# The FFN stage of a BitNet-style transformer layer: the absolute maximum as a tree of max and min, and a subtraction moved from GpSimd to VectorE

## The reference, cut to what matters

```python
def act_quant(x):
    scale = 127.0 / jnp.clip(jnp.max(jnp.abs(x), axis=-1, keepdims=True), 1e-05)
    return jnp.clip(jnp.round(x * scale), -128, 127) / scale
...
h = bit_linear(x, w1)                                  # 1024 -> 4096
h = depthwise_conv1d(h.transpose(0, 2, 1), conv_w, conv_b)   # 3 taps over tokens
h = jax.nn.silu(h.transpose(0, 2, 1))
return bit_linear(h, w2)                               # 4096 -> 1024
...
x = x + _layernorm(_L0_attn_ref(_layernorm(x, axis=-1), ...), axis=-1)
x = x + _layernorm(_L0_ffn_ref(_layernorm(x, axis=-1), ...), axis=-1)
```

## Time and profile before

| | |
|---|---|
| median of 3 runs | 7791.81 us (7787.67 to 7802.6) |
| profiled execution | 7778.59 us, its span 7777.0 us |
| span of the cores | 7753.2 to 7777.0 us |
| mean granted TensorE clock of the cores | 0.695 to 0.699 of full speed |
| busy in the span | PE 48%, PEld 23%, DVE 56%, ACT 15%, POOL 9% |
| DMA, mean over the span | 32 GB/s |

### The profile page before, as it was taken

How to read it: one execution, slowest core, us unless ns; L and a number is a source line. 1 busy time by engine, 2 the same in 40 slices (tenths; PEclk the granted TensorE clock), 3 DMA queues, 4 the chain that set the end, 5 groups by cost and what they waited for, 6 DMA issues and landing times. The chain is left out here.

```text
span 7777.0 us, 57784 instructions; the slowest of 8 cores (7753.2 to 7777.0 us)
## 1 busy us (share of the span) xinstructions
PE 3694.5 (48%) x17510; PEld 1774.1 (23%) x17510; DVE 4360.3 (56%) x5860; ACT 1203.5 (15%) x1194; POOL 674.8 (9%) x630
## 2 busy tenths in 40 slices
PE   0688887221244344344416888872224444344341
PEld 0322222110132222222203222221112232232220
DVE  4344544557666666666653445445546666666665
ACT  0045655000000000000000455650000000000000
POOL 0000000000012112112110000000002112112111
PEclk9987877565566666666658887876656666676665
DMA  6200000113400000000042000001120000000004
GB/s 192 60 6 6 9 9 5 50 38 116 154 6 6 3 6 6 4 6 3 6 154 54 7 7 6 9 12 43 38 98 6 3 6 6 3 6 4 5 6 132
DMA packets 59119, 251.87 MB, mean 32 GB/s; under 512 B 6720, under 2 KB 6848, under 8 KB 55232
## 3 DMA queue, kind: packets, MB, share of 16 engines
q1 hardware_dynamic: 40992, 197.32, 8.1%
q0 software_dynamic: 17824, 50.86, 2.4%
HBM read 185.77 MB, written 67.11 MB: 33 GB/s over the span
## 5 line engine op out<-in xcount | busy, mean ns | idle before, releaser
L851 PE MATMUL s_hps<-s_xqfm,s_w1q 128*128 128x130 bf16 (+1 forms) x8192 | 865.1, 293 | 1143.7 <-DVE s_hgr L863 770.4
L534 ACT ACTIVATE s_pt<-s_sc 128x1024 bf16<-128x1024 f32 x1024 | 1048.9, 1024 | 697.1 <-PE s_sc L521 626.2
L851 PEld LDWEIGHTS s_hps<-s_xqfm,s_w1q 128*128 128x128 bf16 x8192 | 775.4, 134 | 1241.2 <-issue 1220.0
L969 PE MATMUL s_fp<-s_w2q,s_gq 128*128 128x512 bf16 x2048 | 716.7, 513 | 708.6 <-DVE s_gq L958 708.6
L521 PE MATMUL s_sc<-s_qa,s_ka 65*128 65x512 bf16 x2048 | 747.7, 456 | 144.4 <-ACT s_pt L534 25.4
L547 PE MATMUL s_atps<-s_pt,s_vsb 128*65 128x512 bf16 x2048 | 663.1, 420 | 0.0
L900 ACT ACTIVATE s_tcv<-s_tcv 128x4096 bf16<-128x4096 bf16 x32 | 115.7, 3617 | 3448.2 <-DVE s_tcv L898 3448.2
L952 DVE SCALAR_TENSOR_TENSOR s_f<-s_db,s_r 128x512 f32<-128x512 f32 x256 | 395.4, 1545 | 407.3 <-POOL s_db L949 407.3
L940 POOL TENSOR_TENSOR s_yb<-s_tcv,s_sgb 128x512 f32<-128x512 bf16 x256 | 295.9, 1156 | 3534.8 <-DVE s_sgb L926 3502.7
L863 DVE SCALAR_TENSOR_TENSOR s_hgr<-s_hps,iwcol,s_ivfm 128x130 bf16<-128x130 f32 (+1 forms) x1024 | 360.9, 352 | 430.2 <-PE s_hps L851 369.6
L969 PEld LDWEIGHTS s_fp<-s_w2q,s_gq 128*128 128x128 bf16 x2048 | 227.2, 119 | 1184.7 <-issue 1102.5
(11 more groups left out here) (121 smaller groups left out, 3766.9 us busy)
## 6 DMA issues: line engine op xcount, KB each, us to landing
s_xint<-x SPq DMA_DIRECT2D x64, 512.0 KB, 4.1
p0st<-w_t SPq DMA_DIRECT2D x8, 2048.0 KB, 9.0
p0st<-w_t SPq DMA_DIRECT2D x32, 512.0 KB, 3.8
x2scr<-s_x2t SPq DMA_DIRECT2D x32, 512.0 KB, 2.9
s_wst<-w_t SPq DMA_DIRECT2D x16, 1024.0 KB, 5.1
s_wst<-w_t SPq DMA_DIRECT2D x32, 512.0 KB, 3.8
fscr<-s_ft POOLq DMA_DIRECT2D x32, 512.0 KB, 3.0
s_frl<-fscr SPq DMA_DIRECT2D x32, 512.0 KB, 6.0
```

What stands on the lines that cost most here:

```text
L534: em.emit("scalar", lambda e, p=p, j=j: e.activation(pt[:, p * S + j * Q:p * S + (j + 1) * Q], scp[j][:], AF.Exp), waits=w)
L851: j0=j0, j1=j1, t0=t0: e.matmul(ps[:, j0:j1], w1q[:, dc * DH + cc * 128:dc * DH + cc * 128 + 128], xqfm[:, dc * S + t0 + j0:dc * S + t0 + j1],
L969: gq4=gq4, cc4=cc4: e.matmul(ps[:, nb * 512:(nb + 1) * 512], gq4[:, cc4 * 128:(cc4 + 1) * 128], w2q[:, cc * D + nb * 512:cc * D + (nb + 1) ...
```

## The change

Two edits within `_p5_ffn`. The single reduction L902 is replaced by a tree on DVE, once with max into `gmax` and once with min into `f12`, and one operation that joins the two as the larger of the maximum and the negated minimum. The tree works in a new bf16 tile `amx` of 1024 columns. In the quantise loop the difference `db2` is formed by DVE instead of POOL. `yb` gets two buffers, and POOL's multiply of group g waits for DVE's difference of group g - 2, the last reader of that buffer.

```diff
-        nc.sbuf_tensor(f"s{s}_yb", [128, 512], F32) as yb,
+        nc.sbuf_tensor(f"s{s}_yb", [128, 2 * 512], F32) as yb,
...
+        amx_cm = nc.sbuf_tensor(f"s{s}_amx", [128, 1024], BF16)
+        amx = amx_cm.__enter__()
...
-            em.emit("vector", lambda e: e.tensor_reduce(
-                gmax[:], rearr(tcv, "p (c t) -> p t c", c=HC), AX.X, ALU.max,
-                apply_absolute_value=True), waits=[(ac, None)])
+            for op, col in ((ALU.max, 0), (ALU.min, 1)):
+                em.emit("vector", lambda e, op=op: e.tensor_tensor(
+                    amx[:], tcv[:, 0:1024], tcv[:, 1024:2048], op),
+                    waits=[(ac, None)])
+                em.emit("vector", lambda e, op=op: e.scalar_tensor_tensor(
+                    amx[:], tcv[:, 2048:3072], 1.0, amx[:], ALU.mult, op))
+                em.emit("vector", lambda e, op=op: e.scalar_tensor_tensor(
+                    amx[:], tcv[:, 3072:4096], 1.0, amx[:], ALU.mult, op))
+                em.emit("vector", lambda e, op=op: e.tensor_tensor(
+                    amx[:, 0:512], amx[:, 0:512], amx[:, 512:1024], op))
+                em.emit("vector", lambda e, op=op: e.tensor_tensor(
+                    amx[:, 0:256], amx[:, 0:256], amx[:, 256:512], op))
+                em.emit("vector", lambda e, op=op, col=col: e.tensor_tensor(
+                    gmax[:, 0:128] if col == 0 else f12[:, 0:128],
+                    amx[:, 0:128], amx[:, 128:256], op))
+            em.emit("vector", lambda e: e.scalar_tensor_tensor(
+                gmax[:], f12[:, 0:128], -1.0, gmax[:], ALU.mult, ALU.max))
...
-            dg = 0
+            dve_rel = {}
             for g in range(8):
                 gq4 = gqb[:, (g % 2) * 512:(g % 2) * 512 + 512]
+                ybg = yb[:, (g % 2) * 512:(g % 2) * 512 + 512]
                 ts = tcv[:, g * 512:(g + 1) * 512]
-                yw = [(ac, silu_ac), (dv, sgb_dv), (ctx["gc"], dg)]
+                yw = [(ac, silu_ac), (dv, dve_rel.get(g - 2, sgb_dv))]
...
-                em.emit("gpsimd", lambda e: e.tensor_sub(db2[:], yb[:], r02[:]),
-                        inc=ctx["gc"], waits=[(dv, r0d)])
-                dg = ctx["gc"].n
+                em.emit("vector", lambda e, ybg=ybg: e.tensor_sub(
+                    db2[:], ybg, r02[:]))
+                dve_rel[g] = dv.n
                 em.emit("vector", lambda e: e.scalar_tensor_tensor(
-                    f12[:], db2[:], 1.5, r02[:], ALU.is_gt, ALU.add),
-                    waits=[(ctx["gc"], dg)])
+                    f12[:], db2[:], 1.5, r02[:], ALU.is_gt, ALU.add))
```

More of the change, by code:

```diff
@@ L932, in _p5_ffn @@
             silu_ac = ctx["ac"].n
-            dg = 0
+            dve_rel = {}
             for g in range(8):
                 gq4 = gqb[:, (g % 2) * 512:(g % 2) * 512 + 512]
+                ybg = yb[:, (g % 2) * 512:(g % 2) * 512 + 512]
                 ts = tcv[:, g * 512:(g + 1) * 512]
-                yw = [(ac, silu_ac), (dv, sgb_dv), (ctx["gc"], dg)]
+                yw = [(ac, silu_ac), (dv, dve_rel.get(g - 2, sgb_dv))]
                 if i >= 1 and g == 0:
                     yw.append((sf, fspill[i - 1]))
-                em.emit("gpsimd", lambda e, ts=ts: e.tensor_tensor(
-                    rearr_ap3(yb), rearr_ap3(ts), sgv, ALU.mult),
+                em.emit("gpsimd", lambda e, ts=ts, ybg=ybg: e.tensor_tensor(
+                    rearr_ap3(ybg), rearr_ap3(ts), sgv, ALU.mult),
                     inc=ctx["gc"], waits=yw)
                 yg = ctx["gc"].n
-                em.emit("vector", lambda e: e.tensor_copy(qi2[:], yb[:]),
+                em.emit("vector", lambda e, ybg=ybg: e.tensor_copy(qi2[:], ybg),
                         waits=[(ctx["gc"], yg)])
@@ L947, in _p5_ffn @@
                     r02[:], qi2[:], -1.0, None, ALU.add))
-                r0d = dv.n
-                em.emit("gpsimd", lambda e: e.tensor_sub(db2[:], yb[:], r02[:]),
-                        inc=ctx["gc"], waits=[(dv, r0d)])
-                dg = ctx["gc"].n
+                em.emit("vector", lambda e, ybg=ybg: e.tensor_sub(
+                    db2[:], ybg, r02[:]))
+                dve_rel[g] = dv.n
                 em.emit("vector", lambda e: e.scalar_tensor_tensor(
-                    f12[:], db2[:], 1.5, r02[:], ALU.is_gt, ALU.add),
-                    waits=[(ctx["gc"], dg)])
+                    f12[:], db2[:], 1.5, r02[:], ALU.is_gt, ALU.add))
                 ow = []
@@ L988, in _p5_ffn @@
         em.play()
+        amx_cm.__exit__(None, None, None)
     with (
```

## The result

The changed kernel takes 7627.22 us (median of 8 runs, 7624.24 to 7637.09); the kernel before took 7797.2 us in the runs beside it (7773.3 to 7830.93). The ratio is 0.9783, with a 95% interval from 0.9764 to 0.9802: 170 us faster, where 83 were forecast. The profiled executions differ by less, 7778.59 against 7624.8 us or 154 us, and their spans by 7777.0 - 7623.3 = 153.7.

A forecast was written before the change was run, and what follows sets the result against it. DVE's program order plus the POOL handoffs was taken to bound the quantise stretch. Subtraction -174.4, tree +91.5, meetings and clock 0 gave -83 us, so 7791.8 became 7709 us, with 8 in 10 for 7675 to 7770.

The forecast's parts named there:

- What bounds the kernel: FFN tiles: DVE's program order plus the POOL handoffs set the time; shortening that chain shortens the tile one for one.
- Part one: Quantise loop: moving the subtraction from POOL to DVE saves 0.68 us a group, -174 us in all.
- Part two: Quantise loop: two yb buffers change which DVE instruction POOL meets, seven meetings of 0.98 either way, 0 us; lower bound -220.
- rival 4: Quantise loop: meetings get cheaper with DVE ahead, half of the 220 us, giving 7599; chance 0.08.
- rivals in which POOL is shut out (1 and 2): Quantise loop: POOL loses the race now and then (7747, chance 0.15), or every multiply lies bare (7819, chance 0.12).
- rival 1: Quantise loop: POOL is kept out now and then, one of two multiplies lies bare, 38 us more, 7747; chance 0.15.
- Part three: Tile maximum: the tree takes 9.85 us where the reduction took 6.99, +2.86 us a tile, +92 us in all.
- Rival 3: Tile maximum: tree dearer, bf16 min steps at one column a cycle, 30 us more, 7739; both passes 7769; chance 0.05.
- Part four: DVE's wait for the last matmuls of a tile: TensorE's clock effect taken as 0, bounds -19 and +33 us.
- The sum: Whole kernel: -174.4 + 91.5 = -83 us from a median of 7791.8, giving 7709 us; chance 0.58.

The follow-up runs named there:

- three experiments: Old reduction restored in the changed kernel; two-input tree in the one-yb kernel; one-pass absolute-value tree in the changed kernel: 7541.35, 7560.36 and 7481.88 us.
- POOL first again: Changed kernel plus a one-column memset on VectorE between the subtraction and the first scalar-tensor-tensor: 7707.23 us, ratio 0.9893.
- half changes: Two runs: changed kernel with the old single reduction back, 7541.35 us; kernel before with only the tree added, 7880.64 us.
- the quantise loop alone: Changed kernel with the old single reduction back, keeping the subtraction on VectorE and two yb buffers: 7541.35 us, ratio 0.9676.
- the tree alone: Kernel before with the max and min tree in place of the reduction and nothing else: 7880.64 us, ratio 1.0123.
- one yb: Changed kernel with one yb buffer, POOL's multiply of group g waiting for VectorE's subtraction of group g-1: 7640.66 us, ratio 0.9811.
- the multiply on VectorE: Changed kernel with the multiply moved from POOL to VectorE too, POOL left out of the quantise loop: 7642.38 us, ratio 0.9793.

## Why the prediction was wrong

**What bounds the kernel.** Right. What was added to or taken from DVE's chain in the loop came out one for one in the loops' times (146 us for the change with its terms as measured, and 93, 88 and 151 us against 92, 86 and 149 expected for three experiments), but for the wait at the tile's end, which moved by itself.

**Part one, the subtraction.** Right. The last group, which meets nobody, shows it bare: from the cast's start to the end of the second scalar-tensor-tensor 4.02 us before (2746.76 to 2750.78), and 3.35 after (2827.42 to 2830.77). That is 0.67 us, where 0.68 were forecast.

```profile
core 7 of [0, 1, 2, 3, 4, 5, 6, 7], span 7777.0 us
start us, us, engine line op out<-in xcount [idle before <-releaser]
...
2746.76 0.43 DVE L944 CAST s_qi<-s_yb 128x512 int32<-128x512 f32 x1
...
2750.09 0.69 DVE L958 SCALAR_TENSOR_TENSOR s_gq<-s_db,s_f 128x512 bf16<-128x512 f32 x1
...
3430.68 1.16 POOL L940 TENSOR_TENSOR s_yb<-s_tcv,s_sgb 128x512 f32<-128x512 bf16 x1
3431.06 1.32 DVE L952 SCALAR_TENSOR_TENSOR s_f<-s_db,s_r 128x512 f32<-128x512 f32 x1 [1.93 <-POOL s_db L949]
```

(The last two rows are a meeting that part two comes to.)

Over the span it is the 407.3 us that L952 waited, less the 27.4 + 177.2 + 27.3 of the subtraction and the two gaps around it: 175 us.

**Part two, the meetings with POOL: the step that failed.** The prediction said: "If the two exclude each other, the order doesn't change the sum [...] Seven meetings of 0.98 before, seven after: **0 us**." They exclude each other, there are seven before and seven after, and the order does change the sum. Measured from POOL's start, the DVE instruction that it holds up effectively begins after a fixed time (its end less its own unhindered length):

| meeting | POOL's lead | effective start after POOL's start | cost to DVE |
|---|---|---|---|
| before, L952 | 0.03 us | 2719.94 - 0.69 - 2718.23 = 1.02 | 0.98 |
| POOL first again, L969 | 0.16 | 2835.66 - 0.69 - 2833.95 = 1.02 | 0.86 |
| changed kernel, the first cast | 0.20 | 2798.70 - 0.43 - 2797.26 = 1.01 | 0.81 |
| changed kernel, one L968 | 0.33 | 3839.22 - 0.69 - 3837.52 = 1.01 | 0.68 |
| before, one L952 | 0.38 | 3432.38 - 0.69 - 3430.68 = 1.01 | 0.63 |

The cast is met by the second multiply of the row marked x2, which starts 1.15 us before that row's end. The last two meetings are rare ones, in which DVE happened to start later than usual: 8 of the 1536 meetings of groups 2 to 7 on the eight cores of the changed kernel, and 40 of the 1792 meetings before. The one of the kernel before stands in the rows of part one, the one of the changed kernel is this:

```profile
core 5 of [0, 1, 2, 3, 4, 5, 6, 7], span 7623.3 us
start us, us, engine line op out<-in xcount [idle before <-releaser]
...
3837.52 1.16 POOL L957 TENSOR_TENSOR s_yb<-s_tcv,s_sgb 128x512 f32<-128x512 bf16 x1 [2.55 <-DVE s_db L965]
3837.85 1.37 DVE L968 SCALAR_TENSOR_TENSOR s_f<-s_db,s_r 128x512 f32<-128x512 f32 x1 [0.47 <-DVE s_db L965]
```

So POOL ahead costs some 1.01 us less its lead, be it the cast or the first scalar-tensor-tensor that it meets. With DVE ahead, L973's effective start lies 0.87 us behind the end of L968 (2806.60 - 0.69 - 2805.04), and DVE's own gap of 0.105 us is within those 0.87: 0.77. Against the 0.98 of before that is 0.21 us, of which 0.14 is that POOL is further on when it has been held up, and 0.07 is the gap that DVE would have had anyhow. By the rows' totals above that is 45 us in all. DVE first is not cheaper as such: from a lead of some 0.24 us (1.01 - 0.77) on, POOL first costs less, as the rare meeting at 0.33 shows within the changed kernel itself. In the kernel with POOL first again, 16 meetings on the eight cores still had DVE first, and they cost 0.77. With DVE first the instruction met was always the second scalar-tensor-tensor, so that another would lose the same 0.77 isn't shown. The prediction had the ends right (0 to -220) and rival 4 named the direction, at 110 us and 0.08. What it hadn't asked of a held instruction is whether it has already done part of its work when it is let in. That POOL does its first 0.14 us while it waits is an inference from these ends. POOL's own record bears it out: it ends at 2806.06, 1.02 us behind the end of L968, which is 0.14 less than its 1.16. But the profile doesn't show an instruction's inside.

The rivals in which POOL is shut out (1 and 2) fell: POOL got in at the first gap of DVE in every group in which it had work. (The handoff of 0.14 in rival 1 stands in rows 3, not in rows 6, which have 0.22 from L926 to L940.) The Trainium skill (SBUF — State Buffer, Who interferes with whom) says the blocked side waits for the whole instruction. In kind the trace agrees; but the cost here was 0.63 to 0.98 us for a POOL instruction of 1.16, and depended on who was first and by how much. The Trainium skill (SBUF — State Buffer, A bandwidth-pool intuition that's wrong) tells the 115 ns of a GpSimd transfer, not of an instruction like this one. Had they held here too, L973, ready 0.105 us behind L968, would have gone ahead of POOL. It didn't.

**Part three, the tree.** Right: 9.86 us a tile measured, 9.85 forecast, 92 us; 86 and 98 by the medians of the two half changes, 93 and 89 by their loops. Its dear part was named rightly too, the four scalar-tensor-tensor operations: without them 80 us less. Rival 3 fell.

**Part four, TensorE's clock.** Taken as 0 between bounds of -19 and +33, it came out at -18, at the favourable bound. Nothing in the prediction said which way it would go. The eviction's wait fell from 92.3 to 74.7 us in the profiles' slowest cores; over all eight cores it is 91 to 98 before and 75 to 77 after. The half changes say which edit did it: 74 to 75 us with the quantise loop alone, 88 to 96 with the tree alone. The last groups show what went with it. In the tile of the changed kernel shown above the last two follow each other unstretched, 3.45 us apart, and the eight matmuls of each take 1.89 us, the upper of TensorE's two levels. The tile shown of the kernel before ends with 1.89 too, so it is a matter of how often: of 256 evictions on the eight cores 97 waited less than 2.5 us before, and 212 in the changed kernel. In the four kernels with the last two groups unstretched the wait is 73 to 77 us on every core. Where only the last group is unstretched (before, the tree alone, one yb) or all groups are alike (the multiply on VectorE), it is 79 to 98, save two cores of one kernel at 76 and 78. That is a regularity over ten kernels, not a cause shown: no run spaced only the last groups.

**The sum.** 83 + 45 + 18 = 146 us, against 146 in the loops and 154 between the profiled executions. The medians differ by 170. The profiled execution of the kernel before (7778.6) lay near the low end of its runs, the changed kernel's (7624.8) amid its own, and those 16 us are scatter between executions that no run here explains. So of the 87 us between the forecast and the measured gain the meetings hold 45, the clock 18, the stages ahead of the first tile 8 and the scatter 16; the last two, and why the clock went that way, stay open. The range failed by this together: its low end took in the clock's bound but kept the meetings at 0. The meetings alone would have put the forecast at 7709 - 45 = 7664, and that too lies below the range of 7675 to 7770.

## What to carry to other kernels

Read off a meeting of two engines from both sides: what it costs each when it is second, since an instruction that is held can have part of its work behind it, and what counts is who starts first and by how much: here it was cheapest for VectorE to start first, unless GpSimd's lead was over some 0.24 us. Give work to a second engine only if the path's engine doesn't pay for it anyway: here a multiply of 0.80 us with its gap on VectorE was done by GpSimd at a price of 0.77 us to VectorE. And price a tree of operations by the form of each step: at 1024 bf16 columns a scalar-tensor-tensor took 1225 ns and a two-input step 692, and four of the former made the tree slower than the reduction it replaced, while one pass over values with the sign bit cleared made it faster.

## What the runs showed of the hardware that was not expected

- A POOL multiply of 1.16 us costs a DVE instruction 1.01 us less POOL's lead when POOL is first (leads of 0.03 to 0.38 us, on a cast and on a scalar-tensor-tensor), and 0.77 us when DVE is first, and it is then itself 1.67 us long.
- A bitwise and on 16-bit views of 2048 columns takes 694 ns, as fast as the bf16 scaling of 2048 columns in the attention stage (685 ns); min and max of two bf16 tiles take 692 ns at 1024 columns.
- The wait for the last eight matmuls of a tile fell by 15 to 23 us over the kernel on each of the eight cores, without an edit to TensorE's program. It went with the spacing of the groups ahead of them; that the spacing is the cause isn't shown.
